# One pool of PSUM banks for scores, side products and (in the block attentions) the searches for maxima

## The reference

```python
a = softmax(einsum('bshd,bthd->bhst', q, k) * D ** -0.5)
o = einsum('bhst,bthd->bshd', a, v)
```

## Time and profile before

| | us |
|---|---|
| median of 3 runs | 4054.76 |
| the runs | 4044.93, 4054.76, 4060.32 |
| span of the profiled execution | 4044.2 |
| PE busy in it | 3511.0 (87%) |
| DVE, ACT, POOL busy | 2255.6 (56%), 1681.3 (42%), 983.5 (24%) |
| span less `mx`, `a1` and `a2` as cut above | 1495.2 |

### The profile page before, as it was taken

How to read it: one execution, slowest core, us unless ns; L and a number is a source line. 1 busy time by engine, 2 the same in 40 slices (tenths; PEclk the granted TensorE clock), 3 DMA queues, 4 the chain that set the end, 5 groups by cost and what they waited for, 6 DMA issues and landing times. The chain is left out here.

```text
span 4044.2 us, 59055 instructions
## 1 busy us (share of the span) xinstructions
PE 3511.0 (87%) x22156; PEld 2135.3 (53%) x22156; DVE 2255.6 (56%) x4065; ACT 1681.3 (42%) x3067; POOL 983.5 (24%) x1030
## 2 busy tenths in 40 slices
PE   6779999999999884788877689999999996899998
PEld 3433443444443772444546545555555545787877
DVE  6747667577573337544426567676676624534432
ACT  1125646556456231333434135545555553322222
POOL 1200100000000103233333335555555462200000
PEclk9868989999899996898989789999999997999999
DMA  1011211212110311353322244443443402122211
GB/s 68 12 39 45 63 36 45 60 45 51 49 44 23 143 62 42 56 77 62 59 46 76 48 58 63 62 65 56 65 60 58 61 14 77 49 84 63 64 59 61
DMA packets 144627, 229.42 MB, mean 57 GB/s; under 512 B 40916, under 2 KB 90840, under 8 KB 141400
## 3 DMA queue, kind: packets, MB, share of 16 engines
q1 hardware_dynamic: 129048, 216.21, 25.4%
q10 hardware_dynamic: 15296, 9.45, 1.2%
HBM read 99.39 MB, written 8.91 MB: 27 GB/s over the span
## 5 line engine op out<-in xcount | busy, mean ns | idle before, releaser
L940 DVE TENSOR_REDUCE a_mp<-bank 128x1 f32<-128x384 f32 (+2 forms) x1280 | 704.7, 592 | 443.9 <-PE bank L790 429.8
L898 ACT ACTIVATE a_p<-bank 128x512 f32<-128x512 f32 (+1 forms) x1088 | 594.8, 595 | 595.5 <-PE bank L815 523.4
L898 ACT ACTIVATE mx_p<-bank 128x512 f32<-128x512 f32 (+3 forms) x1088 | 548.9, 557 | 471.2 <-PE bank L815 256.2
L940 DVE TENSOR_REDUCE mx_mp<-bank 128x2 f32<-128x768 f32 (+4 forms) x640 | 596.6, 956 | 233.7 <-PE bank L790 143.0
L976 POOL TENSOR_TENSOR a_pair<-a_p 128x512 f32<-128x512 f32 x384 | 491.4, 1310 | 462.0 <-ACT a_p L898 462.0
L790 PE MATMUL bank<-a_ks,a_qs 126*128 126x384 f32 (+2 forms) x1280 | 438.9, 410 | 63.8 <-issue 26.3
L815 PE MATMUL bank<-a_qs,a_ks 128*128 128x512 f32 (+1 forms) x1088 | 421.9, 452 | 41.4 <-DMA a_qs<-a_mt 20.5
L815 PE MATMUL bank<-mx_qs,mx_ks 64*128 64x512 f32 (+3 forms) x1088 | 344.7, 477 | 21.0 <-DMA mx_qs<-mx_mt 13.4
L790 PEld LDWEIGHTS bank<-a_ks,a_qs 126*128 126x128 f32 x1280 | 248.9, 196 | 215.7 <-issue 108.1
L201 POOL TENSOR_TENSOR rs<-ve,neghalf 128x4 f32<-128x4 f32 (+2 forms) x80 | 78.0, 976 | 1168.2 <-DVE ve L196 1125.2
L790 PE MATMUL bank<-mx_ks,mx_qs 62*128 62x384 f32 (+4 forms) x1280 | 314.2, 429 | 7.4 <-DVE mx_mp L940 6.8
(11 more groups left out here) (311 smaller groups left out, 5580.1 us busy)
## 6 DMA issues: line engine op xcount, KB each, us to landing
sf_raw<-in_h_w SPq DMA_DIRECT2D x64, 512.0 KB, 3.5
a_ks<-a_kh SPq DMA_DIRECT2D x96, 192.0 KB, 4.5
ex_w<-in_L_ffn_w SPq DMA_DIRECT2D x16, 1024.0 KB, 5.0
a_qs<-a_qh SPq DMA_DIRECT2D x64, 256.0 KB, 6.1
mx_ks<-mx_kh SPq DMA_DIRECT2D x192, 48.0 KB, 2.1
a_ks<-a_kl SPq DMA_DIRECT2D x48, 192.0 KB, 5.2
mx_qs<-mx_qh SPq DMA_DIRECT2D x128, 64.0 KB, 2.2
mx_rec<-mx_flat SPq DMA_DIRECT2D x128, 64.0 KB, 2.0
```

The lines of the kernel that those rows point to most:

```text
L898: act.activation(probs[place % len(probs)][0:kp, q0:T], self.bank(part, n, kb, h)[0:kp, q0:T], ACT.Exp, scale=scale).then_inc(*self.frees( ...
L940: v.tensor_reduce(best[:, tiled * j:tiled * j + tiled, i, ci], bank[:, 0:w] if tiled == 1 else bank[:, :, 0:w], AX.X, ALU.max).then_inc(*s ...
```

## The change

The banks of the scores and bank 7 become one `Pool`, which is handed to scores and side products alike; in the block attentions the three banks of the searches are in it too. A pool hands out the bank that was given back first in the order of the program, not in time: `back` is called when the instruction that frees a bank is issued. A bank stays out of the pool from its take to that point, which is the same step for scores, searches and most side products, and the later step *split* or *tops_turned* for `q`, `k` and turned maxima. `mx` then has a pool of three banks (4, 5, 7) beside its twins, `a1` and `a2` one of six (0 to 4 and 7). The step "steady" goes.

```diff
@@ class Bank, __init__ @@
         self.tile, self.freed, self.takes = tile, Flag(nc, ctx, f"bank_freed{name}"), 0
+        self.pool = None
...
+class Pool:
+    def __init__(self, banks):
+        self.idle, self.held = list(banks), []
+        for bank in banks:
+            bank.pool = self
+
+    def take(self):
+        bank = (self.idle or self.held).pop(0)
+        self.held.append(bank)
+        return bank
+
+    def back(self, bank):
+        if bank in self.held:
+            self.held.remove(bank)
+            self.idle.append(bank)
...
     def frees(self, *unit):
-        return self.took[unit][0].freed.up()
+        bank, use = self.took[unit]
+        if bank.pool and use == bank.takes:
+            bank.pool.back(bank)
+        return bank.freed.up()
...
         for group in during:
             yield from side(group)
-        yield "steady",
         while found < total[0]:
...
             yield from split(False)
-        yield "steady",
         for group in after:
...
-        a_banks = Ring(self.banks[0:3] if tiled == 1 else self.twins)
-        b_banks = Ring(self.banks[3:5] if tiled == 1 else self.banks[4:6])
-        misc, wide = Ring(self.banks[7:8]), Ring([*b_banks.slots, self.banks[7]])
+        side = Pool([*self.banks[0 if tiled == 1 else 4:5 if tiled == 1 else 6], self.banks[7]])
+        a_banks = side if tiled == 1 else Ring(self.twins)
         d_banks, n_banks = Ring(self.banks[5:6]), Ring(self.banks[6:7])
...
-                    self.take(misc, *unit)
+                    self.take(side, *unit)
...
             elif part == "turn_tops":
-                bank = self.take(misc, part, n)
+                bank = self.take(side, part, n)
...
-                    bank = self.take(b_banks, part, n, kb, h)
+                    bank = self.take(side, part, n, kb, h)
...
-        self.spare = wide
+        self.spare = side
         for part, *at in order():
...
-            elif part == "steady":
-                self.spare = misc if self.spare is wide else wide
             elif part in ATTENTION:
```

## The result

| | before | after |
|---|---|---|
| median of the runs, us | 4057.54 | 3924.14 |
| the runs, from to | 4044.93 to 4061.13 (4) | 3913.16 to 3934.98 (4) |
| ratio, 95% interval | | 0.9679, 0.9652 to 0.9705 |
| span of the profiled execution | 4044.2 | 3911.8 |

What follows compares the result with a forecast made beforehand. PE was taken to bound the three attentions through waits for banks. Kept gains of 42 (`mx`), 23 (`a1`) and 67 us (`a2`) sum to 132: 4044.2 to 3912 us profiled, 3923 us as median; range 3850 to 4042 us.

Steps and rivals of the forecast that it cites:

- What bounds the kernel: In `mx`, `a1` and `a2` PE is the busiest engine by far; time leaves only where it stops stalling or works closer packed.
- No change: Rival: waits move to latency between engines and the DMA of the maxima, under 20 us left, 4040 us; chance 0.11.
- Scores of `mx`: In `mx`, a third bank for scores removes 0.43 of PE's 143.2 us wait for ACT: 62 us.
- Side products of `mx`: In `mx`, side products no longer tied to bank 7 save 0.79 of 27.9 us waiting for DVE: 22 us.
- These halves cannot get shorter: At least 96 halves of `mx` hold two DVE reductions (2.10 us); so half of 84 us is kept, 42.
- Stalls of `a1`: In `a1`, 31 us at side products and 8 at scores, 39 in all, of which 0.6 is kept: 23 us.
- Stalls of `a2`: In `a2`, 64 us at scores and 31 at searches and side products, 95 in all; 0.7 kept, 67 us.
- 54, 63 and 54% busy: Busy shares of ACT, DVE and POOL in `a2`, given beside keeping 0.7 of 95 us there: 67 us.
- New waits: Scores may stand behind reductions (251 in `a1`, `a2`) or side products' readings (100 in `mx`); no sum of their own charged.
- The slower rival: One late reader stops the program-order queue; 20 us slower from 152/351 = 0.43 us per score, 4282 us at full price; chance 0.07.
- The readers as the bound: Rival: ACT and DVE get no faster with more banks, so only 60 us are gained, 3995 us; chance 0.18.
- The swing of the clock: By the skill's rule, `a2` cycling through six banks would fall to clock 0.91 and give back 82 us; not expected.

Runs made afterwards that it cites:

- e1: The changed kernel with the pool in `mx` alone, both block attentions keeping their rings of before: 3979.88 us, ratio 0.9831.
- e6: The changed kernel with four slots each for stacked queries and keys in `a1` (three and five before), steps up to 12 blocks ahead (9 before): 3894.52 us.
- e8: The changed kernel with POOL's additions of pairs of weight blocks in `a2` covering only half of the query columns: 3882.95 us, ratio 0.9579.
- e11: The changed kernel with the pool handing out the bank given back last in program order, not first: 6674.78 us, ratio 1.6482.
- e2: The changed kernel with the pool in the two block attentions alone, `mx` as before: 4005.83 us, ratio 0.9888.
- e4: The changed kernel, but scores take any of three banks, side products bank 7 alone, and searches keep their own banks: 4073.23 us, ratio 1.0055.
- e9: `e6` with the pair additions of every fourth head in `a2` on DVE instead of POOL: 3963.95 us, ratio 0.9788.

## Why the prediction was right, by its steps

- **What bounds the kernel: right.** No engine's work changed and the time left at PE's waits for banks. "No change" is refuted by the ratio; the stages outside moved by no more than 4 us each.
- **Scores of `mx`: nearly right.** The stall counted was 62 us; the subtraction finds 53.7 us at the scores themselves, and 48.0 in `e1`, at the clock of before. The cycle at the end of `mx` fell to 1.11 us, just under the least of 1.13 that the prediction adds up.
- **Side products of `mx`: right.** I counted 22 us; 19.5 were gained at L222 and 3.7 at the turned maxima L801, before what was given back.
- **"These halves cannot get shorter", a half of `mx` kept: the step that failed.** I gave back 42 of 84 us to DVE's double reductions. At the clock of before the stage lost 60 us, so 24 at most were given back, and hardly any of it to DVE. Searches lost nothing: they were issued ahead of need, and DVE, whose idle time before reductions was 233.7 us and is 175.2 now, had room to catch up in other halves. The largest loss, 8.8 to 10.4 us, is at the output projection, whose matmul waits 21.2 instead of 8.4 us for the tile that POOL makes. My working never looked at that wait.
- **The clock of `mx`: a term that the sum lacked.** I expected no loss and thought of no gain. It was granted 0.91 before, and 0.91 to 0.95 with the pool; in the profiled pair the stage gained 80 us and not 60.
- **Stalls of `a1`: nearly right.** 39 us counted, 33.7 gained at side products, scores, turned maxima and transposes. **What took it back: wrong place.** I kept 0.6 because of the maxima sent by DMA; their wait did not change. 21.8 us went to the searches, mostly the first of a job, which wait for stacked queries and keys, and `e6` got them back and 8 us more. Before the change this was, with 26.3 us, already the longest wait of the stage's matmuls, longer than the 16.9 us that I took from the same list; I passed it over because the profile names no releaser for it.
- **Stalls of `a2`: over-counted; the share kept, right.** I counted 95 us and kept 0.7 of them, 67. 53.0 were gained at scores, side products and values, 16.0 given back, so that 37 are 0.7 of what was there. At the end of `a2` the values start 1.06 us sooner of 1.27, a share of 0.83 where I took 0.75 between 0.57 and 1; but that place is not like the stage, in which the scores gained 37.3 us where I had 64. The searches' 18.2 us, which I had taken whole, did not shrink (15.9 us of PE's own and a net loss of 2.8): DVE is late there for another reason, POOL beside it, as `e8` shows.
- **"54, 63 and 54% busy" taken as room: wrong for POOL.** Its additions come in bursts of four (5.10 us) at the pace of the scores. 13.0 us were given back before sums of weights, and ACT waits 43.5 us for POOL instead of 24.4. At the end of `a2` the sign that I gave, ACT fed without a gap of more than 0.6 us, did not come: it stands 2.35 us for POOL.
- **New waits, charged nothing: right.** A score waiting for a reduction appears in `a2` with 1.3 us in 6 waits. Its mirror image I had not named: a search's load waits for an exponential, 17.8 us in 62 waits, of which the matmul itself feels 0.4. The slower rival needed 152 us over 351 scores. It is right as a mechanism though: `e11` has 176 us of that wait in 1900 us.
- **The readers as the bound: false as a whole** (3995 us), true in one place. At the end of `mx` ACT runs nine exponentials in 5.05 us without a gap, so that there a further bank has no gap of ACT left to fill. By the Trainium skill, TensorEngine Tiling (Array Packing), section "PSUM Bottleneck", the emptying of PSUM may become the bottleneck once tiling has made TensorE faster. The trace agrees at this end; over the stage it does not, since ACT still stands idle 403.2 us before exponentials.
- **The swing of the clock: not seen.** The Trainium skill, TensorE: Matmul & The Clock Gate, section "A second HAM failure mode: psum-queue depth-cycling", tells of a kernel that cycles through PSUM banks and whose clock swings by PE's short idles. The trace does not show it here: `a2` cycles through six banks at 0.99, as before, and the 82 us that the prediction worked out for it were not lost. A low clock came where PE waited in nearly every step (`e11`).
- **A slip in the range.** The "some 9 us more" of the lower end is not what it is said to be: with a share of 1 for the scores' 85 us in `a2`, nine tenths kept are 19 us more. The lower end would be 3840 and not 3850 us; nothing hangs on it.

The errors had opposite signs: `mx` was 38 us under-counted, `a1` and `a2` 11 and 30 us over-counted, and the outside moved by -4. The exact hit of 132 us is luck; the sign and the size to within some tens of us are not.

Left open: why the clock of `mx` differs between executions of the same instructions (0.95 and 0.93 with the pool, 0.91 and 0.88 without it), and whether its rise is due to the pool at all. No run here separates that.

## What to carry to other kernels

Where several users write PSUM and each has its own fixed banks, hand all of them one pool and take the bank that was given back first. Neither half of the sharing brought the gain by itself here, and a user that is tied to a bank which others may now take pays for it. When a stall goes, ask in each stage what arrives next (here a DMA of operands issued just in time, and bursts of an engine that is half busy in the mean), since that decides how much is kept; and take the waits without a named releaser into that question. Don't assume that an average engine's slow step bounds its half if the work may slide to the next.

## What the hardware showed that I had not expected

- Two scores on different rows of the array run side by side when both have their bank at once: the pair takes 0.51 us together (0.50 in the earlier trace rows). With the second bank late the second score started behind the first, by 83.0 us in all over 544 pairs before, 38.9 after.
- PE's granted clock does not simply follow how busy it is. In `mx` it was 0.88 at 94% busy (`e2`), 0.91 at 94% (before), 0.95 at 93% (after) and 0.93 at 90% (`e4`); 0.57 came in the stretch of `e11` where PE was busy 67% of the time.
- A piece of a layer norm on DVE (128x128, fp32, SBUF to SBUF) takes 335 ns, and about 1.3 to 1.5 us beside an addition of POOL that takes 1.31 us, while a reduction out of a bank takes 550 ns either way. The additions moved to DVE in `e9` (692 ns at the shortest, 1240 at the median) all ran in part beside one on POOL, so no run shows them alone.
